# State-space layer: dt from one product with W_x W_dt formed on chip, x_dbl cut to B and C; key parts two steps later

## The reference, cut to what matters

```python
xz = rmsnorm(residual) @ W_in;  x, z = split(xz)          # 256 channels each
x = silu(conv(x, conv_w) + conv_b)
x_dbl = x @ W_x                                           # W_x is 256 x 96
dt = softplus(x_dbl[..., :64] @ W_dt + b_dt)              # W_dt is 64 x 256
Bm, Cm = x_dbl[..., 64:80], x_dbl[..., 80:]
h = exp(dt_t * A) * h + (dt_t * x_t) * B_t;  y = sum_n h * C_t   # over 512 tokens, 16 states
out = residual + ((y + x * D) * silu(z)) @ W_out

q, k, v = x @ wq.T, x @ wk.T, x @ wv.T                    # mha: q and k rotated, ALiBi,
out = softmax(q k.T / sqrt(8) + bias, causal) v @ out_w.T + out_b
```

## Time and profile before

| | |
|---|---|
| median of 3 runs | 1346.04 us (1345.93 to 1348.04) |
| profiled execution, its own time | 1347.82 us |
| its span in the profile | 1346.0 us |
| PE busy | 1223.6 us (91%) |
| PEld (weight load, beside PE) | 794.7 us (59%) |
| DVE busy | 908.5 us (67%) |
| ACT busy | 641.6 us (48%) |
| POOL busy | 235.5 us (17%) |
| mean granted clock of PE | 0.958 |

### The profile page before, as it was taken

The page is one execution under the profiler, slowest core; times in us unless marked ns, Lnnn a source line. Parts: engine busy times, 40 slices in busy tenths (PEclk is TensorE's granted clock), DMA queues, the critical chain, the costliest instruction groups (busy, mean ns, idle before and its releaser), DMA issues.

```text
span 1346.0 us, 17205 instructions
## 1 busy us (share of the span) xinstructions
PE 1223.6 (91%) x6152; PEld 794.7 (59%) x6152; DVE 908.5 (67%) x1754; ACT 641.6 (48%) x1183; POOL 235.5 (17%) x201
## 2 busy tenths in 40 slices
PE   5998788899899889799999979789998997989998
PEld 3676444567666555466667744346676664556665
DVE  6765856455467698987765677564555677989765
ACT  4544344534323487862234325444433226969322
POOL 3001000000020065661000010000000101928210
PEclk9999879999999979799999999899999997979999
DMA  6213121000101121220200032200001012212120
GB/s 225 56 32 95 41 57 35 2 1 0 63 1 63 42 69 35 95 95 0 72 24 0 24 88 54 61 4 1 1 1 63 13 51 57 79 57 79 64 71 9
DMA packets 32581, 63.20 MB, mean 47 GB/s; under 512 B 4176, under 2 KB 19824, under 8 KB 32304
## 3 DMA queue, kind: packets, MB, share of 16 engines
q1 hardware_dynamic: 32496, 62.11, 14.7%
HBM read 54.16 MB, written 8.45 MB: 47 GB/s over the span
## 4 chain that ended last, share of the span: by engine, by line
PE 70%; DVE 12%; ACT 9%; DMA 3%; POOL 2%; issue 2%; SPq 1%; DVEq 0%; ACTq 0%; POOLq 0%
PE bank L1519 13%; PE bank L1520 12%; PE bank L1521 12%; PE bank L1688 9%; PE bank L1528 5%; PE bank L1834 3%; DVE a_mx L1400 3%; ACT n_part L1067 3%; PE bank L1597 3%; PE bank L1749 2%; PE bank L1658 2%; ACT n_da L1059 2%; POOL n_hc L819 2%; DMA a_k<-stack_dram 2%; PE bank L1724 2%
## 5 line engine op out<-in xcount | busy, mean ns | idle before, releaser
L1244 DVE SCALAR_TENSOR_TENSOR f_hl<-bank,f_hh 128x512 fp32r<-128x512 f32 x192 | 131.8, 689 | 130.4 <-ACT f_hh L893 129.7
L893 ACT ACTIVATE f_hh<-bank 128x512 fp32r<-128x512 f32 x192 | 114.7, 598 | 188.8 <-PE bank L1597 188.4
L955 ACT ACTIVATE m_sl<-bank 128x512 f32<-128x512 f32 x144 | 86.1, 599 | 235.2 <-PE bank L1521 234.8
L819 POOL TENSOR_TENSOR n_hc<-n_h,n_cs 128x512 f32<-128x512 f32 x128 | 159.9, 1278 | 179.0 <-DVE n_h L1490 172.6
L1519 PE MATMUL bank<-xT_h,mw_h 128*128 128x512 f32 x288 | 161.3, 560 | 3.5 <-DVEq L529 2.7
L1490 DVE TENSOR_TENSOR_SCAN n_h<-n_da,bank 128x512 f32<-128x512 f32 x128 | 149.9, 1207 | 10.0 <-PE bank L1528 7.2
L1688 PE MATMUL bank<-m_h,mw 128*128 128x512 f32 x288 | 145.6, 594 | 0.0
L1400 DVE TENSOR_REDUCE a_mx<-bank 128x1 f32<-128x384 f32 (+3 forms) x176 | 106.2, 637 | 52.6 <-PE bank L1789 50.2
L1311 DVE TENSOR_TENSOR m_t<-m_sl,bank 128x512 f32<-128x512 f32 x128 | 87.9, 687 | 78.4 <-PE bank L1521 77.3
L1834 PE MATMUL bank<-n_hc,ident 128*128 128x512 f32 x256 | 136.1, 619 | 0.2
L973 ACT ACTIVATE a_p<-bank 128x1024 f32<-128x1024 f32 (+3 forms) x128 | 87.8, 703 | 91.7 <-PE bank L1726 90.7
(11 more groups left out here) (241 smaller groups left out, 2362.7 us busy)
## 6 DMA issues: line engine op xcount, KB each, us to landing
n_cs<-c_dram SPq DMA_DIRECT2D x32, 512.0 KB, 3.6
m_c<-comb_dram SPq DMA_DIRECT2D x28, 512.0 KB, 5.1
a_q<-stack_dram SPq DMA_DIRECT2D x8, 512.0 KB, 4.2
a_k<-stack_dram SPq DMA_DIRECT2D x16, 256.0 KB, 5.2
stage_fw<-in_fw_dram SPq DMA_DIRECT2D x6, 512.0 KB, 7.0
stack_dram<-R SPq DMA_DIRECT2D x16, 192.0 KB, 2.8
w_stage<-in_mw_dram SPq DMA_DIRECT2D x9, 256.0 KB, 2.7
stack_dram<-R SPq DMA_DIRECT2D x16, 128.0 KB, 2.6
```

The lines of the kernel that those rows point to most:

```text
L819: n_hcs.by(nc.gpsimd.tensor_tensor(n_hc[:, i % 4, :], n_h[:, i % 4, :], n_cs[:, j % C_RING, i // 2 % 2, :], ALU.mult))
L1244: f_lo.by(V.scalar_tensor_tensor(f_h[1][:, i % 4, :], bank[:, i % 3, :], 0.0, f_h[0][:, i % 4, :].bitcast(F32), ALU.max, ALU.subtract))
```

## The change

Four parts.

1. W_x[:, :64] W_dt, a 256 x 256 matrix, is formed on chip once: two more loads (`wdt` and `wxT`, 64 x 256 each, 64 KB) in SP's queue ahead of batch 1, two products on PE into bank 7 at step 2 of the first tree unit, a copy to `wxd` on ACT at step 3, PE's wait for it at step 4. `wdt` leaves the small loads.
2. In a state-space unit dt comes straight from `n_xc` by four products of 512 columns with `wxd`; x_dbl follows, of 32 rows only. ACT's copy of the 64 rows is gone. In the second slot gathers 30 and 31 stand ahead of dt. The exponential is taken by halves, each behind its |v|. DVE's order stays as it was; it waits for the second half of the exponential where it waited for the whole.
3. In a first slot the last turn (i = 31) comes ahead of the next slot's first two projections, and gather 26 behind them.
4. When the attention's first slot makes the second slot's parts, the stages from 15 on come two steps later: keys at 17, 18, 19 on ACT, residuals at 17 and 18 on DVE.

```diff
+KEYS_LATER = 2
...
         for own, ahead in ((DVE_STAGES, HEAD_DVE_STAGES), (ACT_STAGES, HEAD_ACT_STAGES), (PE_STAGES, HEAD_PE_STAGES)):
             if table is own:
+                if host == "mha":
+                    ahead = {n + KEYS_LATER * (n >= 15): name for n, name in ahead.items()}
                 return ahead.get(i)
...
-        wdt = sb("wdt", [64, NHALF, P])
+        wxd = sb("wxd", [P, NHALF, NHALF * P])
...
+        wdt, wxT = (spare[0:64, n * NHALF * P:(n + 1) * NHALF * P] for n in (4, 5))
...
             tree_weights(0, 1)
+            load(wdt, A["wdt"], wdt_in)
+            load(wxT, A["wxT"], wdt_in)
             batch(1)
...
+                    if u == 0 and i == 3:
+                        act.wait_ge(w_xd.sem, w_xd.at(0, 0))
+                        w_xds.by(act.activation(flat(wxd[:]), bank[:, 7, :], ACT.Copy))
...
                 act.activation(preload, half[:, 0, 0:NT], ACT.Exp)
-                act.wait_ge(n_xdb.sem, n_xdb.at(k, 0))
-                n_dtc.by(act.activation(n_dtr, bank[0:64, 4, :], ACT.Copy))
                 for m in range(2):
                     act.wait_ge(n_dtp.sem, n_dtp.at(k, m))
                     n_abss.by(act.activation(n_abs[:, m, :], bank[:, m, :], ACT.Abs, bias=b_dt[:, m:m + 1]))
-                act.wait_ge(n_abss.sem, n_abss.at(k, 1))
-                n_us.by(act.activation(n_u, n_abs, ACT.Exp, scale=-1.0))
-                act.wait_ge(n_us.sem, n_us.at(k, 0))
+                    act.wait_ge(n_abss.sem, n_abss.at(k, m))
+                    n_us.by(act.activation(n_u[:, m], n_abs[:, m], ACT.Exp, scale=-1.0))
                 for m in range(2):
+                    act.wait_ge(n_us.sem, n_us.at(k, m))
                     n_lns.by(act.activation(n_ln[:, m], n_u[:, m], ACT.Ln, bias=1.0))
...
-                dve.wait_ge(n_us.sem, n_us.at(k, 0))
+                dve.wait_ge(n_us.sem, n_us.at(k, 1))
...
+                    if u == 0 and i == 2:
+                        pe.wait_ge(wdt_in, 32)
+                        for m in range(NHALF):
+                            ins = mm(bank[:, 7, m * NHALF * P:(m + 1) * NHALF * P], wxT[:, m * P:(m + 1) * P], wdt,
+                                     start=True, stop=True)
+                        w_xd.by(ins)
+                    if u == 0 and i == 4:
+                        pe.wait_ge(w_xds.sem, w_xds.at(0, 0))
...
-                for m in range(2):
-                    pe.wait_ge(n_sil.sem, n_sil.at(k, 2 - p + m))
-                    ins = mm(bank[0:96, 4, :], wx[:, m, :], n_xc[p][:, m, :], start=m == 0, stop=m == 1)
-                n_xdb.by(ins)
                 if p == 1:
                     gather(k - 1, last - 1)
                     gather(k - 1, last)
-                pe.wait_ge(n_dtc.sem, n_dtc.at(k, 0))
+                for half in range(NHALF):
+                    for m in range(2):
+                        if half == 0:
+                            pe.wait_ge(n_sil.sem, n_sil.at(k, 2 - p + m))
+                        ins = mm(bank[:, half, :], wxd[:, m, half * P:(half + 1) * P], n_xc[p][:, m, :],
+                                 start=m == 0, stop=m == 1)
+                    n_dtp.by(ins)
                 for m in range(2):
-                    n_dtp.by(mm(bank[:, m, :], wdt[:, m, :], n_dtr, start=True, stop=True))
+                    ins = mm(bank[64:96, 4, :], wx[:, m, 64:96], n_xc[p][:, m, :], start=m == 0, stop=m == 1)
+                n_xdb.by(ins)
...
                 for i in range(2, last + 1):
-                    back_to_scan(k, p, i)
-                    if p == 0 and i >= last - 1:
-                        if i == last - 1:
-                            ready(u + 1)
-                        project(k + 1, 1, i + 1 - last)
+                    if p == 1 or i < last:
+                        back_to_scan(k, p, i)
+                    if p == 0 and i == last - 1:
+                        back_to_scan(k, p, last)
+                        ready(u + 1)
+                        project(k + 1, 1, 0)
+                        project(k + 1, 1, 1)
                     if i >= 4:
                         gather(k, i - 4)
```

More of the change, by code:

```diff
@@ L340, in program @@
         n_brow = n_cs[:, 2, 0, :]
-        n_dtr, n_crow, n_db = n_hc[0:64, 0, :], n_hc[:, 1, :], n_hc[:, 2:4, :]
+        n_crow, n_db = n_hc[:, 1, :], n_hc[:, 2:4, :]
         n_abs, n_u, n_ln, n_sq = n_h[:, 0:2], n_h[:, 2:4], n_da[:, 0:2], n_da[:, 2:4]
@@ L360, in program @@
         bias_in = sem("bias_in")
+        wdt_in = sem("wdt_in")
         fw_in = [sem(f"fw_in_{n}") for n in range(2 * TREES)]
@@ L457, in program @@
         a_out = sig("a_out", "mha", 1)
+        w_xd = sig("w_xd", "once", 1)
+        w_xds = sig("w_xds", "once", 1)
         n_in = sig("n_in", "mamba", 4)
@@ L465, in program @@
         n_xdb = sig("n_xdb", "mamba", 1)
-        n_dtc = sig("n_dtc", "mamba", 1)
         n_btp = sig("n_btp", "mamba", 1)
@@ L473, in program @@
         n_abss = sig("n_abss", "mamba", 2)
-        n_us = sig("n_us", "mamba", 1)
+        n_us = sig("n_us", "mamba", 2)
         n_lns = sig("n_lns", "mamba", 2)
@@ L564, in program @@
         block = ctx.enter_context(nc.Block())
-        NSMALL, NEARLY = 10, 4
+        NSMALL, NEARLY = 9, 4
         @block.sync
@@ L653, in _ @@
                     tree_weights(t, which)
-            small = [(t[:], name) for t, name in ((owT, "owT"), (wx, "wx"), (wdt, "wdt"), (wout, "wout"),
+            small = [(t[:], name) for t, name in ((owT, "owT"), (wx, "wx"), (wout, "wout"),
                                                   (amat, "a_log"), (gate_b, "gate_b"), (tri, "tri"),
@@ L2025, in layouts @@
     d["wx"] = a["L1_attn_W_x"].reshape(NHALF, P, 96).transpose(1, 0, 2)
-    d["wdt"] = a["L1_attn_W_dt"].reshape(64, NHALF, P)
+    d["wdt"] = a["L1_attn_W_dt"]
+    d["wxT"] = a["L1_attn_W_x"][:, 0:64].T
     d["wout"] = a["L1_attn_W_out"].reshape(NHALF, P, P).transpose(1, 0, 2)
```

## The result

| | before | changed |
|---|---|---|
| median of 20 runs each | 1346.32 us | 1350.7 us |
| ratio of the runs (20 and 18) | | 1.0024, 95% interval 1.0016 to 1.0033 |
| profiled execution, span | 1347.82, 1346.0 | 1353.55, 1351.8 |

Two of the changed kernel's 20 runs were slow (2066.07 and 2459.9 us); the ratio leaves them out, and the median of the other 18 is 1349.9.

The account below looks back on a forecast made before the run. PE was taken to bound most of the kernel (70% of the chain), with DVE's written order setting dt at state-space starts; +0.9 + 6.5 - 2.4 = +5.0 us on the median 1346.04 gave 1351.0 us, range 1346.0 to 1355.0.

Parts of the forecast that it names:

- dt from one product: State-space starts: correction term later by 0.2 and 0.7 in first slots, 2.8 in each second slot; +6.5 us.
- L1456 is what is late next: State-space start: the C-row copy on DVE waits for x_dbl, 3.4 later in first slots, 2.8 in second, others queued behind.
- Setup: First tree unit: two on-chip weight products add 0.86 us on PE; loads and ACT's eviction cost 0.
- Halves, C rows, last turn: Exponential by halves, later copy of C rows in state-space starts, and scan 31's turn moved ahead: each 0 us.
- Keys: Attention: key stages two steps later give -1.7 us in the first pair, -0.7 in the second; -2.4 together.
- -0.7**, and the load and PE follow: Second pair's attention: SP's key writes start 0.7 us earlier, and the key load and PE move with them.
- Sum: Whole kernel: +0.9 + 6.5 - 2.4 = +5.0 us, put on the median: 1351.0 us.
- The attention pays for the rest: No-change rival: first pair keeps full clock, second escapes its half clock; +0.6, 1346.6 us; chance 0.15.
- DVE ready first: Rival at state-space starts: dt comes 1.5 earlier in each of four, 1338.5 us; chance 0.01, counted with faster.

Follow-up runs that it names:

- dt alone: The kernel before with the on-chip weight product and dt from it; exponential whole, last turn and keys as before: 1354.29 us, ratio 1.0053.
- dt-first kernel: The changed kernel with DVE's order turned: gated products, n_pos, correction term, then the wait for x_dbl and the copies: 1340.31 us, ratio 0.995.

## Why the prediction was right, step by step

- **dt from one product: +6.5 forecast, 7.2 by the profile's places, 7.1 by the run of dt alone.** L1456 came 3.58 later in first slots (forecast 3.44) and 2.89 in second slots (2.8), counted from the convolution; the correction term +0.42, +0.98 and twice +2.9 (0.2, 0.7, 2.8). Three small things were short. The 1.72 for x_dbl was read from a chain in which PE itself goes on, so that its last pass ends where the next begins; DVE waits for that pass to its end, 1.85. From the copy to the correction term a first slot took 2.24, not 2.1. And the forecast took before's two first slots as they stood, one of them with B products at half clock. That L1456 is what is late next, with everything behind it, is shown by two runs that changed DVE's order alone. The sum went by DVE not passing a waiting instruction; DVE idled 4.65 with gated half 1 ready behind it. By the rule of the Trainium skill (TensorE: Matmul & The Clock Gate, "Architectural detail", engine queue depths), strictly first in, first out on VectorE, it must be so, and the trace agrees: with the same product written ahead of the wait, it ran some 5.4 earlier, counted from the convolution, right behind the first one, and the correction term 1.4 earlier. The forecast had put that alternative at 1.3 in each second slot.
- **Setup: +0.86 forecast, +0.3 by the runs (-1.1 to 1.6), about 1.25 by the place.** The passes were priced by columns at 0.86 and took 1.13. In the changed profile the part up to the sixth eviction grew by 1.41; of the 0.86 that was there at the first eviction, 0.32 was left at the third, before the first new product.
- **Halves, C rows, last turn: 0 forecast, 0.3 and 0 measured.** ACT was earlier, and it bought nothing while DVE waited for x_dbl. In the dt-first kernel ACT's halves do lead the path. What they are worth there was not tried; the exponential ended 0.4 earlier in each start with them (changed kernel with keys not later, against dt alone), so 1.7 at most is an estimate.
- **Keys: -2.4 forecast, -4.0 measured on this kernel (uncertain by 2; -7.3 on the one before).** This is the term that was most mis-sized. The mechanism held: key writes 3.4 earlier on the clock, 4.5 counted from the attention's start (forecast 3.9); 0.95 in the second pair (forecast 0.7); a wait of 3.19 and 2.73 for the keys in both pairs, with half clock behind it. What failed is the step "**-0.7**, and the load and PE follow": the second attention became 2.6 shorter, with 8.4 us at half clock instead of 12.0. I had left its clock as it was; with later keys only the shorter of its two lengths occurs, and before's profile happened to have the longer. The first pair, -1.24 in this profile against -1.7 forecast, averages -2.9 over seven.
- **Sum: +5.0 forecast, +3.2 measured (2.2 to 4.4).** The keys' term gave 1.6 more than forecast, the state-space term took 0.7 more and by the place the setup 0.4 more, so the errors cancel in part; that the sum came out this near is partly luck. The parts run alone add up to about 0 (7.1 - 7.3 + 0 + 0.3) against 3.2 for the whole. Their intervals, added in squares, come to some 3 either way, so this gap is not settled; with the mean of 5 for the keys the sum would be 2.4.
- **The rivals.** "The attention pays for the rest" would have been 1346.6: right in direction, too large on this kernel. "DVE ready first" was put at 1338.5, with each start 1.5 ahead of before, and all but excluded by DVE's order as written; with the order turned the correction terms were 2.1, 1.0, 1.6 and 1.0 ahead and the time 1340.3. The kernel with the later keys alone is as fast, so that time is no sign that the dt product pays.

## What to carry to other kernels

A shorter chain on one engine pays only if the engine that joins the results takes them in the new order; after moving a product, look for the idle time that the joining engine has ahead of its first wait, and what stands behind it ready. Before moving an instruction behind the path's start, ask what the engines beside it allow in return: the same move gave 10 us in one kernel and cost 2 in the other. When a copy or a product seems later, ask from which instruction it was counted: behind an earlier neighbour everything seems late. Where the clock makes one stretch come out in two lengths, size a term there from several profiles, not from one.

## What the runs showed that I had not expected

The product of 32 output rows costs what that of 96 costs. The chains seem to say 1.85 against 1.72, but they end the two differently; PE's timelines, second slot of the changed kernel and of before, have the four passes level:

```profile
534.78 1.91 PE L1901 MATMUL bank<-n_part,wx 128*32 128x512 f32 x4
```

```profile
529.24 1.88 PE L1871 MATMUL bank<-n_part,wx 128*96 128x512 f32 x4
```

One pass is 592 ns in the median of 16 in both kernels. And a stretch of the same instructions, the second attention with the keys where they were, differed by 3.7 us between profiled executions (+0.30 to -3.43), with 12.0 and 8.1 us of it at half clock.
